# Another order of the work in a step of the router stage, with small operations moved, merged and an output layout changed

## What is computed

```python
# x: (32, 128, 32, 32); v = layernorm of x over the 128 channels of each pixel
a = mean(v, pixels) @ w1.T + b1;  m = max(v, pixels) @ w2.T + b2     # per image
taps = softmax(m - a over the 9 taps of a 3x3 kernel, per channel)
x = x + (depthwise_conv3x3(v, taps) + bias + v)                       # per image and channel
t = tokens of x                                                       # 32768 tokens of 128
n = layernorm(t)
top_w, top_i = top_k(n @ Wg + bg, 2);  top_w = softmax(top_w)         # 8 experts
out = t + sum over the 2 chosen e of w_e * (gelu(n @ W1[e] + b1[e]) @ W2[e] + b2[e])
```

## Time and profile before

| | |
|---|---|
| Median of 3 runs | 1751.96 us (1745.91 to 1754.96) |
| Profiled execution | 1765.64 us, its span 1763.9 us |
| PE busy | 1534.5 us (87% of the span) |
| DVE busy | 1373.4 us (78%) |
| ACT busy | 1059.2 us (60%) |
| POOL busy | 993.0 us (56%) |

### The profile page before, as it was taken

How to read it: one execution, slowest core, us unless ns; L and a number is a source line. 1 busy time by engine, 2 the same in 40 slices (tenths; PEclk the granted TensorE clock), 3 DMA queues, 4 the chain that set the end, 5 groups by cost and what they waited for, 6 DMA issues and landing times.

```text
span 1763.9 us, 45712 instructions
## 1 busy us (share of the span) xinstructions
PE 1534.5 (87%) x12190; PEld 1137.3 (64%) x12191; DVE 1373.4 (78%) x2855; ACT 1059.2 (60%) x2331; POOL 993.0 (56%) x1061
## 2 busy tenths in 40 slices
PE   4799888888798836899999999999999999999655
PEld 2344444544454421788888888888888888888644
DVE  1578878678778873788888888888889888888634
ACT  3577656556557520677777777777777777776300
POOL 1004545334455464577777777777777777777400
PEclk9899889889889855899999999999999999999866
DMA  3201211111121013211111111111111111110299
GB/s 123 72 26 59 64 59 61 50 60 49 52 68 59 30 40 119 64 41 43 42 44 46 41 38 43 38 44 42 41 44 41 45 41 44 46 40 8 71 360 332
DMA packets 90599, 115.79 MB, mean 66 GB/s; under 512 B 15278, under 2 KB 71754, under 8 KB 90551
## 3 DMA queue, kind: packets, MB, share of 16 engines
q1 hardware_dynamic: 65752, 62.29, 12.6%
q0 software_dynamic: 18176, 34.27, 6.1%
q10 hardware_dynamic: 6624, 18.69, 2.7%
HBM read 60.22 MB, written 58.61 MB: 67 GB/s over the span
## 4 chain that ended last, share of the span: by engine, by line
POOL 33%; issue 23%; PE 17%; DVE 11%; ACT 7%; DMA 4%; POOLq 1%; SPq 1%; another core or an unknown queue 1%; DVEq 0%; ACTq 0%
POOL xn L462 13%; POOL token_out L474 12%; POOL yt L469 8%; PE psV L752 6%; PE psV L710 4%; DMA ye<-token_out 4%; DVE x L1014 3%; PE psT L737 3%; PE psG L739 2%; ACT spent L560 2%; PE psA L701 1%; ACT lnv L528 1%; ACT sd L532 1%; ACT sq L537 1%
## 5 line engine op out<-in xcount | busy, mean ns | idle before, releaser
L1210 DVE TENSOR_TENSOR gl<-g,gh 128x512 f16<-128x512 f32 x624 | 477.9, 805 | 107.2 <-ACT gh L646 101.8
L450 POOL DMA_INDIRECT rows_by_pair<-rows,idx x256 | 273.8, 1070 | 407.0 <-issue 274.2
L474 POOL DMA_INDIRECT token_out<-yt,rt x312 | 340.3, 1091 | 186.5 <-POOL yt L469 132.7
L646 ACT ACTIVATE gh<-g 128x512 f16<-128x512 f32 x468 | 276.1, 624 | 17.2
L752 PE MATMUL psV<-lp,diag 128*128 128x512 f32 x512 | 260.4, 639 | 23.3 <-ACT cv L553 12.6
L639 ACT ACTIVATE g<-psV 128x512 f32<-128x512 f32 x312 | 184.9, 597 | 139.2 <-PE psV L858 121.8
L462 POOL TENSOR_SCALAR xn<-rt 128x128 f32<-128x128 f32 x312 | 240.3, 776 | 27.1 <-DMA rt<-rows_by_pair 23.6
L639 ACT ACTIVATE g<-psT 128x512 f32<-128x512 f32 x312 | 183.3, 597 | 110.7 <-DVE gl L1210 67.2
L879 PE MATMUL psR<-wall,gh 128*128 x1248 | 223.9, 274 | 18.5 <-issue 9.9
L879 PE MATMUL psG<-wall,gh 128*128 x1248 | 223.0, 273 | 0.0
L880 PE MATMUL psG<-wall,gl 128*128 x1248 | 214.3, 219 | 0.0
(11 more groups left out here) (220 smaller groups left out, 3063.9 us busy)
## 6 DMA issues: line engine op xcount, KB each, us to landing
rt<-rows_by_pair SPq DMA_DIRECT2D x156, 133.0 KB, 2.1
xb<-in_x_dram SPq DMA_DIRECT2D x32, 512.0 KB, 3.3
ye<-token_out SPq DMA_DIRECT2D x32, 512.0 KB, 9.9
out_dram<-oe ACTq DMA_DIRECT2D x32, 512.0 KB, 6.1
token_out<-yt,rt POOLq DMA_INDIRECT x312
rows_by_pair<-rows,idx POOLq DMA_INDIRECT x256
stage<-in_L_ffn_W_dram SPq DMA_DIRECT2D x1, 2048.0 KB, 8.2
rows_by_pair<-pad_rows SPq DMA_DIRECT2D x15, 133.0 KB
```

The lines of the kernel that those rows point to most:

```text
L450: gp.indirect_dma_start(rows_dram, bass.IndirectOffsetOnAxis(ap=idx[p][:, b:b + 1].bitcast(U32), axis=0), rows[p][:, b, :], None).then_inc ...
L474: gp.indirect_dma_start(y_dram, bass.IndirectOffsetOnAxis(ap=rt[r][:, b, ID:ID + 1].bitcast(U32), axis=0), yt[r][:, b, :], None, bounds_ch ...
L646: sc_.activation(gh[side][q][:, cols], g[side][:, cols], ACT.Copy).then_inc(hi_act, 1)
L1210: v.tensor_tensor(gl[side][q][:, cols], g[side][:, cols], gh[side][q][:, cols], ALU.subtract).then_inc(lo_done, 1)
```

## The change

The two kernels compute the same. Parts of it:

1. **Order.** In every engine's `step` the pieces stand in another order. VectorE runs image 1's five window operations in one piece at the step's start, selects the best expert (`first_choice`) ahead of `norm` of image 0 and the second one behind it, runs four of image 0's five window operations ahead of `norm` of image 1, and has the taps' softmax and `shifts` ahead of the fifth, with `weigh` behind it. TensorE does all tap products in one piece (they lay between other matmuls before), `centre` of image 1 ahead of `turn` where it stood behind the convolution before, and one convolution matmul as the step's last. ScalarE interleaves `token_squares` with `inv_std`.
2. **Moved from VectorE to ScalarE.** The two negated means (`means`, now `token_means`) and the doubled deviation in the row (`RSTD`).
3. **Merged.** Two `shifts` into one; the two routing weights come from one Exp over two exponents (`gaps`) and one multiplication into both columns; the absolute value and the conversion of the row numbers are one operation. The chain of stage 4 has 24 links, 30 before.
4. **Output rows by partition.** `token_out` holds token (partition p, block b) of an image in row 8p+b; before it was row 128b+p.

The core of the diff:

```diff
-                sp.dma_start(ye[j][:, :, :], y_dram.rearrange("(n b p) d -> n p b d", b=NBLK, p=P)[bass.ds(n, 1)].rearrange("a p b d -> (a p) b d")).then_inc(ye_in[j], 16)
+                sp.dma_start(ye[j][:, :, :], y_dram.rearrange("(n p b) d -> n p b d", b=NBLK, p=P)[bass.ds(n, 1)].rearrange("a p b d -> (a p) b d")).then_inc(ye_in[j], 16)
...
-                gp.iota(rows[p][:, :, ID].bitcast(I32), [[P, NB2]], base=(2 * p - 4) * PIX, channel_multiplier=1)
+                gp.iota(rows[p][:, :, ID].rearrange("p (k b) -> p k b", k=2).bitcast(I32), [[PIX, 2], [1, NBLK]], base=(2 * p - 4) * PIX,
+                        channel_multiplier=NBLK)
...
+            def token_means(st_, k):
+
+                act.wait_ge(tok_ready, st_.count(3, 2, k + 1))
+                if not st_.fixed or st_.count(3, 1, 0) > 0:
+                    act.wait_ge(lg_ready, st_.count(3, 1, 0))
+                sc_.activation(negm[st_.slot(3)][:, k * NBLK:(k + 1) * NBLK], psG[:, 0:NB2 * G].rearrange("p (b g) -> p b g", g=G)[:, k * NBLK:(k + 1) * NBLK, E],
+                               ACT.Copy, scale=-1.0).then_inc(stat_ready, 1)
...
-                sc_.activation(rows[p][:, k * NBLK:(k + 1) * NBLK, 0:D], psT[:, :].rearrange("p (b d) -> p b d", d=D), ACT.Copy, scale=0.5).then_inc(kept, 1)
+                blks = slice(k * NBLK, (k + 1) * NBLK)
+                sc_.activation(rows[p][:, blks, 0:D], psT[:, :].rearrange("p (b d) -> p b d", d=D), ACT.Copy, scale=0.5)
+                act.wait_ge(rstd_ready, st_.count(3, 2, k + 1))
+                sc_.activation(rows[p][:, blks, RSTD], rstd[p][:, blks], ACT.Copy, scale=2.0).then_inc(kept, 1)
...
-                link(v.tensor_scalar(den[:, :], e2[:, :], WSCALE, WSCALE, ALU.mult, ALU.add))
-                link(v.reciprocal(wa[:, :], den[:, :]))
-                link(v.tensor_tensor(wb[:, :], e2[:, :], wa[:, :], ALU.mult))
...
+                link(v.tensor_tensor(den[:, :], e2[:, :, 0], e2[:, :, 1], ALU.add))
+                link(v.reciprocal(wa[:, :], den[:, :]))
+                dve.wait_ge(kept, st_.count(4, 2, 2))
+                v.scalar_tensor_tensor(out=r_[:, :, W_LO:W_HI + 1], in0=wa[:, :].unsqueeze(2).broadcast_to([P, NB2, 2]), scalar=1.0 / WSCALE, in1=e2[:, :, :],
+                                       op0=ALU.mult, op1=ALU.mult)
+                v.tensor_scalar(r_[:, :, NMR], nmr[st_.slot(4)][:, :], 1.0, None, ALU.add)
```

More of the change, by code:

```diff
@@ L566, in token_std, with expose @@
                 sc_.activation(rstd[st_.slot(3)][:, k * NBLK:(k + 1) * NBLK], tln[:, :], ACT.Exp, scale=-0.5).then_inc(rstd_ready, 1)
+            def expose(st_):
+                act.wait_ge(gap_ready, st_.count(4, 1, 1))
+                sc_.activation(e2[:, :, :], gaps[:, :, :], ACT.Exp).then_inc(e2_ready, 1)
             def keep(st_, k):
@@ L579, in step @@
                     diagonals(st_, 0)
[L580 to L602, removed]
@@ L603, in step @@
-                if st_.next().on(1):
-                    square(st_.next(), 0)
+                    diagonals(st_, 1)
+                if st_.on(1):
+                    inv_std(st_, 0, 0)
+                if st_.on(3):
+                    token_means(st_, 0)
+                    token_squares(st_, 0, 0, NBLK)
+                if st_.on(2):
+                    take(st_, 0, 0)
+                if st_.on(3):
+                    token_std(st_, 0)
+                if st_.on(1):
+                    inv_std(st_, 0, 1)
@@ new lines, in step @@
+                if st_.on(3):
+                    keep(st_, 0)
+                if st_.on(2):
+                    take(st_, 0, 1)
+                if st_.on(1):
+                    sum_up(st_, 0)
+                    square(st_, 1)
+                if st_.on(4):
+                    expose(st_)
+                if st_.on(3):
+                    token_means(st_, 1)
+                    token_squares(st_, 1, 0, NBLK // 2)
+                if st_.on(1):
+                    inv_std(st_, 1, 0)
@@ L605, in step @@
+                if st_.on(3):
+                    token_squares(st_, 1, NBLK // 2, NBLK)
+                if st_.on(1):
+                    inv_std(st_, 1, 1)
+                if st_.on(3):
+                    token_std(st_, 1)
+                if st_.on(2):
+                    take(st_, 1, 0)
+                if st_.on(1):
+                    sum_up(st_, 1)
+                if st_.on(3):
+                    keep(st_, 1)
                 if st_.on(1):
@@ L608, in step @@
                     sc_.activation(ez[:, :, :], zd[:, :, :], ACT.Exp).then_inc(ez_ready, 1)
+                if st_.next().on(1):
+                    square(st_.next(), 0)
+                if st_.on(2):
+                    take(st_, 1, 1)
                 if st_.first:
@@ L775, in step @@
                 if st_.first:
-                    for h in range(2):
-                        centre(st_, 0, h)
+                    centre(st_, 0)
                 for k in range(2):
+                    if k == 1 and st_.on(1):
+                        centre(st_, 1)
                     if st_.on(3):
@@ L1004, in add_image, with window @@
                 v.tensor_tensor(x1[j][:, :], cv[k][:, :], xb[j][:, :], ALU.add).then_inc(x_used, 1)
-            def window(st_, stage, k, part):
+            def window(st_, stage, k, first, end):
                 j, n = 2 * st_.slot(stage) + k, st_.count(stage, 2, k)
-                if part == 0:
+                if first == 0:
                     c_win.begin(n)
                     dve.wait_ge(x_used, n + 1)
-                for m in (range(2 + k), range(2 + k, len(DVE_TAPS)))[part]:
+                for m in range(first, end):
                     dy, dx = divmod(DVE_TAPS[m], 3)
```

194 lines of the change are left out of this document (92 added, 102 removed).

## The result

| | before | changed |
|---|---|---|
| Median (4 runs each) | 1748.93 us (1745.84 to 1754.96) | 1779.31 us (1773.67 to 1784.76) |
| Profiled execution, its span | 1765.64, 1763.9 us | 1784.76, 1783.0 us |
| First part (to TensorE's first tile of the second part) | 712.2 us | 745.2 us |
| Second part | 956.2 us | 955.4 us |
| Third part | 95.5 us | 82.4 us |

What follows compares the result with a forecast made beforehand. No engine was full; a ring of waits between VectorE, TensorE and ScalarE set the first part's step. 65 us less there and 13 in the third part made 78 less, 1752 - 78 = 1674 us, range 1652 to 1706.

Steps and rivals of the forecast that it cites:

- The new order: First part, changed order of a step: the two long waits go, 30.8 us a step, taken as 31.2 with the scatter.
- the walk: First part: one step followed through the hand-written order with measured durations; 35.6 us before, 31.2 with the change.
- the marks named: Signs of being right: `norm` of image 0 31 us apart, idle under 0.5, variances 1.1, clock 0.97 or more, third part 87.
- The wait of `keep` for the scatter: First part, ScalarE: `keep` of image 0 waits about 3 us for GpSimd's scatter in the changed order.
- The loop's own stall: First part, even loop steps: TensorE waits 2.63 us, VectorE 1.36; kept as 4.3 us in each of four steps.
- Third part: Output stage: loads in 4096-byte pieces at 47.2 engine-us per MB instead of 60.3, 13 us less.
- the 19 of the bound: Third part: upper bound of its gain, 19 us less if loads cost the stores' 40.5 engine-us per MB.
- The overlap of 1.07: Third part: packets of two queues overlap by 1.07, so (792 + 680)/16/1.07 = 86 us.
- The rule of the Trainium skill (DMA: Bandwidth & Descriptors, Specifications): Third part: full rate at pieces from 512 bytes up, so loads gain nothing; rival at 1687 us, chance 0.13.
- Slower: Rival, first part: same ring of waits with scatters of 30 us and more, up to 1770 us; chance 0.03.
- over 4: Sign of being wrong: ScalarE's `keep` waits over 4 us for the scatter.

Runs made afterwards that it cites:

- pause10: The changed kernel, with GpSimd waiting for the signal of image 1's turn ahead of piece 10 of 16 of each scatter; 1674.24 us, 0.954 of before.
- pause12: The changed kernel, with GpSimd waiting for the signal of image 1's turn ahead of piece 12 of 16 of each scatter; 1700.05 us, 0.9672 of before.
- layout: The kernel before with the new layout of the output rows alone (part 4 of the change); 1733.0 us, 0.9904 of before.
- before_delay6: The kernel before, with six memsets of a spare tile on GpSimd (6 to 7 us) ahead of each scatter; 1818.89 us, 1.0354 of before.
- turn_behind: The changed kernel, with TensorE's turn of image 1 behind both variances and ScalarE's means and squares behind both inverse deviations; 1756.26 us, 1.004 of before.

## Why the prediction was wrong

**The step that failed** is in "The new order": the walk lets each engine start when the instruction it waits for has ended by its row. For the turn of image 1 that is wrong by 6.5 to 7.6 us, since its signal comes that late beside the scatter. "TensorE idles 0.9 us there instead of 2.47, and in no place over 1 us. So the clock stays at the upper level" fell with it: TensorE waits 6.79 us ahead of the second variance of image 1, and the clock falls as in the earlier trace rows. `norm` of image 1 came 6 us late, and the rest of the step with it. 39.9 - 31.2 = 8.7 us a step over eleven to twelve steps is 96 to 104 us, the 105 between 1674 and 1779.

**The walk itself was right but for that.** With the signal prompt (`pause10`) the step is 31.2 us, the number forecast, though GpSimd's wait makes a scatter 2 to 3 us longer there. Of the marks named, most are met: `norm` of image 0 31 us apart, the mean clock 0.99, variances at 1.1; VectorE idles 0.2 to 0.5 us ahead of `norm` of image 0 in all full steps but one (0.99), and the third part is 82.3 us, not 87. That the median is 1674.24 and the forecast 1674 is luck in part: the forecast kept 17 us for the loop's stalls (4 x 4.3), which `pause10` doesn't have, and it was made for profiled executions, where it had 78 us less and these show 93 (1765.64 to 1672.77). By the ratio it is 0.046 x 1750 = 81 us less. The wait of `keep` for the scatter was sized well too (3.14 us). Of the 81, 17 are the layout's and 28 the merged operations', by the middle of wide intervals; the other 35 are left for the order and the moved means, once the turn's signal isn't late.

**The loop's own stall was misread.** The earlier trace rows show TensorE waiting 2.63 us for "remote" and VectorE stopping 1.36 us between two of its own linked operations, both in the two microseconds around the end of a scatter (the last piece of the earlier trace rows ends at 461.83). That is what the late signals look like in `pause12` too. I put it down to the loop, and kept 4.3 us for it in four steps. `layout` has the loop of the kernel before unchanged, and in its profile no step of the loop is over 37.1 us, where the kernel before has 40.9 to 42.8 in the four even ones; that is what its mean step is shorter by (34.8 against 37.3). In `pause10`, with a loop of the same length in turns and steps, no wait for "remote" is left between 150 and 600 us, and no step of the loop is over 32.0 us, odd or even. The Trainium skill's rule of a stall at a taken branch (Runtime: NRT & Kernel Launch, Instruction fetch mechanics) seemed to fit; by it the stall would be in both kernels, and the measurement decides against it as the cause of the earlier trace rows. That the stall of the earlier trace rows is a late signal is argued from its place and its look; no run removed it alone. A second sign stood in the trace of before, in a draining step with little else going on: the turn's last product ends at 637.89, VectorE is free at 639.17, and reads it at 641.40, 0.2 us behind the last piece.

```profile
637.46 0.43 PE L739 MATMUL psG<-wgc,x 128*128 128x9 f32 x2
...
638.97 0.20 DVE L1034 TENSOR_TENSOR nmr<-negm,rstd 128x8 f32<-128x8 f32 x1
...
640.24 0.96 POOL L450 DMA_INDIRECT rows_by_pair<-rows,idx  x1 [0.30 <-issue]
641.40 0.17 DVE L1028 TENSOR_SCALAR negm<-psG 128x8 f32<-128x8 f32 x1 [2.23 <-remote]
```

In the old order the full steps' turn of image 1 came beside or behind the last piece, so it was late by 1.9 us at most. The new order moved it some 8 us forward in the scatter (its end from 22 to 27 us behind the first piece's start to 15 to 18), and no term of the sum asked what it moved beside.

**Third part.** 13.1 us less, as forecast, but by luck: two errors cancel. In 1710 to 1780 us the queues show:

```profile
q10 hardware_dynamic: 4302, 15.69, 54.8%
q1 hardware_dynamic: 3713, 13.50, 47.4%
```

A load costs 0.474 x 16 x 70 / 13.50 = 39.3 engine-us per MB, and not 47.2 (60.3 before); that alone would have given the 19 of the bound. The overlap of 1.07 is nearly gone, though: the two queues add up to 1.02, and the DMA share is 0.99. The rule of the Trainium skill (DMA: Bandwidth & Descriptors, Specifications) that would have made the gain 0 doesn't hold here, by the 13 us.

**The rivals.** "Slower" was priced at 1755 to 1770 with a chance of 0.03, by scatters of 30 us and more. The time came out on its side, but the scatters took 21 to 22 us, as before: the right sign by another mechanism. `keep` of image 0 waits 1.7 to 4.4 us in the full steps of the changed kernel and 1.8 to 4.3 in those of `pause10`, so the mark "over 4" didn't tell the cases apart. The layout and the third part gave nothing of the miss.

## What to carry to other kernels

A wait for "remote" of some microseconds is a finding, and not noise to be carried over: look what GpSimd and the transfers do at its end, and whether it always ends with them. When an order is changed, ask for each short piece on the critical path what it will now run beside, and not only what it waits for. If a signal comes late beside a long run of indirect transfers, a wait that parts the run around it can be worth more than it costs (here 105 us, for 2 to 3 us more of scatter).

## What the hardware showed beyond that

- TensorE's signal of the turn was up to 8.0 us late beside GpSimd's indirect scatter (9.4 with two products), in the new order and in the old one; in `pause12` one of VectorE's signals to itself came 2.7 us late at the same time, and beside 32 pieces without a wait nearly every one came 1.2 us late from piece 12 on. In the changed kernel and in `before_delay6` the turn's signal came 1.0 to 2.6 us behind the end of the last piece, in `pause12` 1.7 to 2.3 us behind the last piece ahead of the wait. TensorE's rows don't show it. The Trainium skill (Perfetto Trace Analysis, Tensor Engine Instruction) says that the end of a TensorE row is an estimate, and that the semaphore is pushed only when PSUM has acknowledged the bytes. That place is hidden in a row, and the trace agrees that what is late lies behind the row's end; it doesn't show that it is the acknowledgement, and VectorE's late signals come from operations that write no PSUM.
- Why the pieces do this stays open. Shown is what it is not: the semaphore's place, the data that the turn reads, the product that signals, VectorE's small operations beside it, the waiting engine. A scatter issued from another queue, or one without landings to count, wasn't tried. That a variance beside piece 12 was prompt in `turn_behind`, where a turn is late in the changed kernel, has no explanation here.
